# An attention and feed-forward block on one core: products moved in the steps of the last batch, the first transfers reordered

## The reference

```python
pos = 1.0 + x * (1.0 + 0.5 * x * (1.0 + x / 3.0))
neg = 1.0 / (1.0 - x * (1.0 - 0.5 * x * (1.0 - x / 3.0)))
s = where(x >= 0, pos, neg); attn = s / sum(s)     # x = logits - max(logits)
...
h = _layernorm(x) * (1 + ca) + sa
x = x + ga * attn(h)                               # q, k, v of 16 heads; times w_out, plus b_out
h = _layernorm(x) * (1 + cb) + sb
h = concat([h, -h]); h = relu(s0 * (h @ W0)) * 2   # 256 -> 512
h = relu(s1 * (h @ W1)) * 2                        # 512 -> 512
x = x + gb * s2 * (h @ W2)                         # 512 -> 128
```

## Time and profile before

| | before |
|---|---|
| median of 3 runs | 696.83 us (695.08 to 698.17) |
| profiled execution | 694.62 us, span 692.7 us, so 1.9 us lie outside the span |
| PE busy | 632.7 us (91%), 3065 matmuls |
| DVE busy | 641.2 us (93%), 757 instructions |
| ACT busy | 601.9 us (87%) |
| POOL busy | 598.8 us (86%) |
| DMA | 53.62 MB |

### The profile page before, as it was taken

The page is one execution under the profiler, slowest core; times in us unless marked ns, Lnnn a source line. Parts: engine busy times, 40 slices in busy tenths (PEclk is TensorE's granted clock), DMA queues, the critical chain, the costliest instruction groups (busy, mean ns, idle before and its releaser), DMA issues.

```text
span 692.7 us, 9651 instructions
## 1 busy us (share of the span) xinstructions
PE 632.7 (91%) x3065; PEld 253.7 (37%) x3065; DVE 641.2 (93%) x757; ACT 601.9 (87%) x622; POOL 598.8 (86%) x394
## 2 busy tenths in 40 slices
PE   6767998899889998999989998999989999998998
PEld 4223333334223343234423342234423343334366
DVE  6889999999999999999999999999999999998853
ACT  2587898998999989999999989998999989998932
POOL 8759888899989999999989999999989899797810
PEclk9588999999999999999999999999999999999999
DMA  8423112522214122512214122512214122101001
GB/s 230 159 67 132 53 51 61 168 63 59 63 53 154 32 58 72 174 55 59 77 47 156 37 58 70 176 55 59 75 51 160 32 58 72 52 10 28 16 13 31
DMA packets 37783, 53.62 MB, mean 77 GB/s; under 512 B 11308, under 2 KB 20804, under 8 KB 37732
## 3 DMA queue, kind: packets, MB, share of 16 engines
q1 hardware_dynamic: 36748, 51.81, 24.8%
q10 hardware_dynamic: 984, 1.19, 0.5%
HBM read 29.17 MB, written 18.36 MB: 69 GB/s over the span
## 4 chain that ended last, share of the span: by engine, by line
PE 56%; DVE 23%; issue 10%; ACT 9%; DMA 1%; ACTq 1%; DVEq 0%
PE MB L525 13%; PE OP L603 12%; DVE mx L988 11%; PE Z L571 9%; DVE cub L979 9%; PE SA L586 8%; ACT sq L736 4%; PE MB L538 3%; PE MB L515 2%; ACT prob L750 2%; PE MB L496 1%; ACT hid L843 1%; PE MB L503 1%; ACT hid L791 1%; DMA KH<-SK 1%
## 5 line engine op out<-in xcount | busy, mean ns | idle before, releaser
L1227 POOL TENSOR_TENSOR cub<-cub 128x2048 f32<-128x2048 f32 x127 | 456.8, 3603 | 39.7 <-DVE cub L979 39.4
L736 ACT ACTIVATE sq<-Z,shift 128x1024 f32<-128x1024 f32 x256 | 282.2, 1116 | 43.3 <-PE Z L571 41.8
L979 DVE SCALAR_TENSOR_TENSOR cub<-sq,Z 128x1024 f32<-128x1024 f32 x256 | 309.5, 1210 | 11.0 <-ACT sq L736 10.8
L988 DVE TENSOR_REDUCE mx<-SA 128x2 f32<-128x1024 f32 x248 | 301.7, 1216 | 13.4 <-PE SA L586 9.9
L750 ACT ACTIVATE prob<-cub 128x2048 f32<-128x2048 f32 x128 | 244.4, 1910 | 1.5 <-DVE cub L946 1.1
L586 PE MATMUL SA<-KH,QL 64*128 64x512 f32 x496 | 123.0, 492 | 30.9 <-DVE mx L988 25.3
L571 PE MATMUL Z<-QH,KH 64*128 64x512 f32 x512 | 128.9, 500 | 5.9 <-DVE cub L979 5.8
L603 PE MATMUL OP<-prob,Vq 128*16 128x512 f32 x1024 | 134.3, 598 | 0.0
L571 PEld LDWEIGHTS Z<-QH,KH 64*128 64x128 f32 x512 | 48.2, 185 | 181.8 <-DVE cub L979 124.1
L525 PE MATMUL MB<-hid,W 128*128 128x512 f32 x192 | 108.1, 645 | 0.0
L586 PEld LDWEIGHTS SA<-KH,QL 64*128 64x128 f32 x496 | 47.4, 187 | 111.5 <-DVE mx L988 85.1
(11 more groups left out here) (215 smaller groups left out, 522.5 us busy)
## 6 DMA issues: line engine op xcount, KB each, us to landing
QL<-parts_q SPq DMA_DIRECT2D x62, 128.0 KB, 2.6
KH<-parts_k SPq DMA_DIRECT2D x62, 128.0 KB, 2.7
QH<-parts_q SPq DMA_DIRECT2D x62, 128.0 KB, 2.7
parts_q<-SQ SPq DMA_DIRECT2D x28, 256.0 KB, 2.6
parts_k<-SK SPq DMA_DIRECT2D x28, 256.0 KB, 2.7
nd<-OT SPq DMA_DIRECT2D x124, 32.0 KB
QH<-mp SPq DMA_DIRECT2D x126, 4.0 KB
out<-y SPq DMA_DIRECT2D x7, 256.0 KB, 2.8
```

Of the source, the lines that this page charges most:

```text
L736: nc.scalar.activation(sq[:, h, :], Z[:, h, :], ACT.Square, bias=shift[:, 0:1]).then_inc(s_sq, 1)
L979: nc.vector.scalar_tensor_tensor(cub[:, m % RING, h, :], sq[:, h, :], CUB_ADD, Z[:, h, :], ALU.add, ALU.mult).then_inc(s_cv, 1)
L988: nc.vector.tensor_reduce(to, unit_bank(m, u)[:, :, :], AX_X, ALU.max).then_inc(s_mx, 1)
L1227: nc.gpsimd.tensor_tensor(ff, ff, ff, ALU.mult).then_inc(s_fp, 1)
```

## The change

In the lead-in: x is loaded in four parts in place of three, and the third (batches 4 and 5) moves behind the first quad and the writing of the parts of q, the fourth (6 and 7) behind the reading of quad 1. The first quad's QH transfers move ahead of the writing of q's parts. ACT waits for the parts of x one by one as it sums, leaves its two DMAs of the first rows of maxima to SP, and squares tiles in steps -2, -1, 2 and 3 in place of -3 to 0. POOL's `norms_of_x` of these moves from step 3 to step 5. PE gets 14 more matmuls without a reader before the first logits, and fills in steps 10 to 12 of the lead-in.

In the last batch's steps: the first layer of batch 6 is made in steps 11 and 12 (before 11 to 14), two of its products in banks of SA; the second layer in steps 13 to 15, its last product in steps 128 and 129 as before; half of `y` in step 130, before in the tail. Transposes of `h2T` move to the start of step 11, and DVE's `norm_late` to the end of its step. DVE reads out the first layer in steps 11 to 14 (before 12 to 15), and the last square is done half by DVE in step 127 and half by POOL. A fill less is made among the logits' fills.

```diff
--- before.py
+++ after.py
@@ -56,8 +56,8 @@
 AV_BEHIND = 5
 LOADS = 4
 ON_VECTOR = 3
-SQUARES_AT = (-3, -2, -1, 0)
-X_LOADS = (slice(0, 1), slice(1, 4), slice(4, B))
+SQUARES_AT = (-2, -1, 2, 3)
+X_LOADS = (slice(0, 1), slice(1, 4), slice(4, 6), slice(6, B))
 M_DMAS = 4
 LEAD = 3
 FIRST = -1
@@ -89,30 +89,31 @@
     ("l1_3", -2, [(6, "c", 1), (6, "d", 1), (7, "c", 1), (7, "d", 1)]),
     ("x1", -1, [(8, "b", 2), (8, "c", 2)]),
     ("y", -2, [(9, "b", 1), (9, "c", 1), (9, "d", 1), (10, "b", 1)]),
-    ("h2T", -1, [(10, "d", 4)]),
-    ("l0_0", -1, [(11, "c", 4)]), ("l0_1", -1, [(12, "c", 4)]), ("l0_2", -1, [(13, "c", 4)]), ("l0_3", -1, [(14, "c", 4)]),
-    ("l1_0", -1, [(13, "d", 1), (14, "d", 1), (15, "d", 1), (H, "c", 1)]),
-    ("l1_1", -1, [(13, "d", 1), (14, "d", 1), (15, "d", 1), (H, "c", 1)]),
+    ("h2T", -1, [(11, "a", 4)]),
+    ("l0_0", -1, [(11, "c", 4)]), ("l0_1", -1, [(11, "d", 4)]), ("l0_2", -1, [(12, "c", 4)]), ("l0_3", -1, [(12, "d", 4)]),
+    ("l1_0", -1, [(13, "c", 2), (14, "b", 1), (15, "b", 1)]),
+    ("l1_1", -1, [(14, "c", 2), (14, "d", 1), (15, "c", 1)]),
+    ("l1_2", -1, [(15, "c", 2), (15, "d", 2)]),
 ]
 
 MISC[B] = [
-    ("l1_3", -2, [(0, "b", 3), (0, "c", 1)]), ("l1_2", -2, [(2, "c", 4)]), ("y", -2, [(5, "c", 3), (5, "d", 1)]),
+    ("l1_3", -2, [(0, "c", 4)]), ("y", -2, [(2, "d", 2), (5, "c", 1), (5, "d", 1)]),
 ]
 
 
 
-FILL = {(FIRST, n): ("v", 1) for n in range(13, 16)}
+FILL = {(FIRST, n): ("v", 1) for n in range(10, 16)}
 FILL |= {(0, n): ("k", 2) for n in range(2, 11)} | {(0, n): ("v", 2) for n in range(12, 16)}
 FILL |= {(1, n): ("k", 3) for n in range(2, 8)} | {(1, n): ("x1", 1) for n in range(9, 11)} | {(1, 12): ("v", 3)}
 
-FILL_LOGITS = {(B - 1, n) for n in (10, 11, 12)}
+FILL_LOGITS = {(B - 1, 9), (B - 1, 10)}
 
 
 MAIN_AT = {"xbg": 6, "wog": 5, "den_sq": 6, "den_inv": 6, "att": 7, "st2": 9, "mv2": 10, "rs2": 11, "x1n": 11,
            "w2g": 0, "xn": 10}
 AT = {b: MAIN_AT for b in range(FIRST, B)}
 AT[B - 1] = MAIN_AT | {"st2": 9, "mv2": 9, "rs2": 9, "x1n": 10}
-AT[B] = MAIN_AT | {"xbg": 0, "wog": 0, "w2g": 1}
+AT[B] = MAIN_AT | {"w2g": 0, "xbg": 1, "wog": 1}
 
 
 
@@ -356,8 +357,10 @@
 
         own_bank = {product(FIRST, "k", 0): (SA[:, 0, :], None),
                     product(B - 1, "y", B - 3): (SA[:, 1, :], None),
-                    product(B - 1, "l1_0", B - 2): (SA[:, 0, :], None),
-                    product(B - 1, "l1_1", B - 2): (SA[:, 1, :], product(B - 1, "y", B - 3)),
+                    product(B - 1, "l0_1", B - 2): (SA[:, 0, :], None),
+                    product(B - 1, "l0_2", B - 2): (SA[:, 1, :], product(B - 1, "y", B - 3)),
+                    product(B - 1, "l1_0", B - 2): (SA[:, 0, :], product(B - 1, "l0_1", B - 2)),
+                    product(B - 1, "l1_1", B - 2): (SA[:, 1, :], product(B - 1, "l0_2", B - 2)),
                     product(B, "l1_3", B - 2): (Z[:, 1, 0:S], None),
                     product(B, "y", B - 2): (SA[:, 1, :], product(B - 1, "l1_1", B - 2))}
         common = [o for o in order if o not in own_bank]
...
@@ -577,6 +580,7 @@
                     return
                 beta, g, r, qt = logits_at(m, u)
                 if m == 0 and u == 0:
+                    without_reader(14)
                     pe.wait_ge(s_gate, 1)
                 if m % QUAD == 0 and u == 0:
                     pe.wait_ge(s_qk[g], loads_of_qk(beta, g) * 16)
@@ -621,7 +625,10 @@
             scores(s + 1, 0)
             misc("a")
             logits(m, 1)
-            with_v(s)
+            if s != GROUPS:
+                with_v(s)
+            if s == GROUPS - 1:
+                with_v(s + 1)
             misc("b")
             scores(s + 1, 1)
             misc("c")
@@ -670,7 +677,7 @@
                 if t % 2 == 1:
                     mm.then_inc(t_x1, 1)
             y_before = product(B, "y", B - 2)
-            misc_product(pe, *y_before, range(0, 3))
+            misc_product(pe, *y_before, range(2, 3))
             for t in range(TB):
                 pe.wait_ge(t_x1n, t + 1)
                 mm = nc.tensor.transpose(t_h2T_banks[t // 2][:, t % 2 * P:(t % 2 + 1) * P], x1n[:, t, :], ident[:, :])
@@ -740,7 +747,7 @@
                     if m < GROUPS - 1:
                         act.wait_ge(s_fp, m + 1)
                     else:
-                        act.wait_ge(s_last_fp, 1)
+                        act.wait_ge(s_last_fp, 2)
                     if m == 0:
                         act.wait_ge(s_wts, 2)
                         act.wait_ge(s_W0, 2)
@@ -827,14 +834,12 @@
                 write_parts(nc.scalar, "k", 0, OTHER_QUADS)
             if b == FIRST and n == 3:
 
-                for load in s_x[1:]:
-                    act.wait_ge(load, 16)
                 for i in range((B - ON_VECTOR) * TB):
+                    for j, load in enumerate(X_LOADS):
+                        if i == 0 and j == 1 or i == (load.start - ON_VECTOR) * TB:
+                            act.wait_ge(s_x[j], 16)
                     mm = nc.scalar.activation(scratch(i), tile_of_x(i), ACT.Copy, accum_out=sum1[:, i:i + 1])
                 mm.then_inc(s_sum1, 1)
-            if s == 4 - AHEAD:
-                act.wait_ge(s_mp, 1)
-                rows_of_maxima(nc.scalar, 0, range(2, P // 32))
             if s in SQUARES_AT:
                 if s == SQUARES_AT[0]:
                     act.wait_ge(s_mean1, 1)
@@ -941,8 +946,9 @@
             ones(KH, slice(1, 2))
 
         def last_square(dve):
+
             dve.wait_ge(s_cv, 2 * GROUPS)
-            ff = cub[:, (GROUPS - 1) % RING].rearrange("p a n -> p (a n)")
+            ff = cub[:, (GROUPS - 1) % RING, 1, :]
             nc.vector.tensor_tensor(ff, ff, ff, ALU.mult).then_inc(s_last_fp, 1)
 
         def sums_of(dve, quad):
@@ -1052,32 +1058,31 @@
             if m > QUAD:
                 of_maxima(m, 1)
             split(b, n)
-            if b == B - 1:
-                norm_late()
             cubic(s, 1)
             if m > QUAD:
                 of_maxima(m, 2)
             maxima(m, 1)
             if b < B - 1:
                 norm_sums()
+            else:
+                norm_late()
             if b == B - 1 and n in (8, 12):
                 sums_of(dve, (s - AV_BEHIND) // QUAD)
-            if b == B - 1 and n >= 12:
-                take_late(dve, b, f"l0_{n - 12}")
             if b == B - 1 and n == 11:
                 dve.wait_ge(s_made["y"], B - 2)
                 dve.wait_ge(s_out, 16 * (B - 3))
                 nc.vector.tensor_tensor(flat(y), bank_of(*product(b, "y", B - 3))[0], flat(xs[:, B - 3]), ALU.add)\
                     .then_inc(s_y, 1)
+            if b == B - 1 and 11 <= n < 15:
+                take_late(dve, b, f"l0_{n - 11}")
+            if b == B - 1 and n == 15:
+                last_square(dve)
             if b == B and n in (0, 4):
                 sums_of(dve, (s - AV_BEHIND) // QUAD)
             if b == B and n == 0:
-                last_square(dve)
-                take_late(dve, B - 1, "l1_0")
-                take_late(dve, B - 1, "l1_1")
+                for name in ("l1_0", "l1_1", "l1_2"):
+                    take_late(dve, B - 1, name)
                 take_late(dve, B, "l1_3")
-            if b == B and n == 2:
-                take_late(dve, B, "l1_2")
             if b == FIRST and n == 2:
                 stats_of_x(dve, 1)
                 means_of_x(dve, 1)
@@ -1221,7 +1226,11 @@
             b, n = s // H, s % H
 
             def square_of(m):
-                if 0 <= m < GROUPS - 1:
+                if m == GROUPS - 1:
+                    pool.wait_ge(s_cv, 2 * m + 1)
+                    ff = cub[:, m % RING, 0, :]
+                    nc.gpsimd.tensor_tensor(ff, ff, ff, ALU.mult).then_inc(s_last_fp, 1)
+                elif 0 <= m < GROUPS:
                     pool.wait_ge(s_cv, 2 * (m + 1))
                     ff = cub[:, m % RING].rearrange("p a n -> p (a n)")
                     nc.gpsimd.tensor_tensor(ff, ff, ff, ALU.mult).then_inc(s_fp, 1)
@@ -1301,7 +1310,7 @@
                 normalise_x(b + 2)
             if at(s, "x1n", -1, b, n) and b < B - 1:
                 normalise_x1(b - 1)
-            if b == 0 and n == 3:
+            if b == 0 and n == 5:
                 norms_of_x(pool, True)
             square_of(s)
 
@@ -1349,7 +1358,6 @@
             sp.dma_start(k0u, k0.rearrange("(a p) n -> p a n", p=P)).then_inc(ld_k, 16)
             sp.dma_start(k1u, k1.rearrange("(a p) n -> p a n", p=P)).then_inc(ld_k, 16)
             sp.dma_start(k2u, k2.rearrange("(a p) n -> p a n", p=P)).then_inc(ld_k, 16)
-            load_x(sp, 2)
         def sp_step(sp, s):
             b, n = s // H, s % H
 
@@ -1368,8 +1376,9 @@
                 if beta == 0:
                     sp.wait_ge(s_zero, 2)
                     first_quad(sp, QL, "q", s_qk[0])
+                    first_quad(sp, QH, "q", s_qh[0])
                     write_parts(sp, "q", 0, OTHER_QUADS)
-                    first_quad(sp, QH, "q", s_qh[0])
```

(4 more changed lines are left out.)

4 lines of the change are left out of this document (2 added, 2 removed).

## The result

The changed kernel takes 703.47 us in the median of 4 runs (702.89 to 706.65), the kernel before beside it 696.03 (695.08 to 698.17). The ratio is 1.0103 with a 95% interval of 1.0078 to 1.0128: slower by 1.0%, and outside the predicted range. The profiled execution has a span of 701.1 us, 692.7 before. PE is busy for 641.6 us, 632.7 before, DVE for 644.7, 641.2 before.

What follows compares the result with a forecast made beforehand. No one engine bounds the whole, its 128 steps run in series; at the end PE's own work bounds. Lead-in 0 and end +0.9 on 694.62 gave 695.5, plus 2.2 for the median: 697.7 us, range 694.0 to 700.8.

Steps and rivals of the forecast that it cites:

- x1n at 633.9 ... the first cubic of step 12 ... 2.1 us late: Last batch: x1n ends at 633.9 after POOL's square; DVE waits for l0_0, so that cubic starts at 641.5, before 639.38.
- The slower rival: Last batch: POOL's next square breaks up x1n, 2.4 us on top, +3.3 in all, 700.1 us; chance 0.2.
- PE's own work: The end: from step 15's values' product PE is the bound, 12.5 us to the last values' products, 11.8 before.
- the sum: Whole kernel: lead-in about 0 and end +0.9 us added to the profiled 694.62 us, giving 695.5; 697.7 for the median.
- 1.71 us of PE go for sure: The end: PE's wait of 1.71 us at 644.27 for a first-layer bank to be read out goes.
- the faster rival: Lead-in and end: x early or gate rows not delaying quad 2, end gaps closed; -2.7 us, 694.1 us; chance 0.2.
- gain of 0.2: Tail: y matmuls shrink to a third, but what follows waits for x1n on DVE, so only 0.2 us gained.
- 1.0 without cover: Last square: halving it gains nothing as PE is the bound behind it; without PE's cover it would give 1.0 us.
- The fills cost nothing: Lead-in: two pairs of logits at 0.43 and a fill of some 1.05 us stand against two maxima of 1.13 each.
- ten late squares: Lead-in, ACT: squares moved to steps 2 and 3 cost 0.2 us in step 2 and 1.3 more in step 3.
- its own bounds (-0.9 to +2.4): Lead-in: -0.9 us if x lands after 2.7 us, +2.4 if after 6.0 and nothing else gives way.
- its bound of 3.0: The end: 3.0 us later if y's two thirds and the 2.1 us late first cubic of step 12 add up.

Runs made afterwards that it cites:

- norm_early: Changed kernel with DVE's norm_late back ahead of the second cubic of its step, nothing else: 701.59 us, 1.0067.
- last_steps_only: Changed kernel with all lead-in edits undone, the last batch as changed: 701.49 us, 1.0065.
- both_mended: Changed kernel with x1n early, read-outs behind steps 12 and 13's cubics, y in the tail, q's parts ahead of QH, gate rows behind quad 2's read-back: 696.21 us.
- lead_parts_first: Kernel before with the lead-in's edits alone, but q's parts written ahead of the first quad's QH, as before: 698.74 us, 1.0028.
- lead_thin: As lead_parts_first, with the gate rows' write one step later and the ten late squares spread two in each of steps 2 to 6: 695.2 us, 0.9979.
- all_thin: As both_mended, with the ten late squares of x spread two in each of steps 2 to 6: 693.79 us, 0.9964.

## Why the prediction was wrong

**The forecast took the wrong case at x1n.** Its step was "x1n at 633.9 ... the first cubic of step 12 ... 2.1 us late", blocked by one square of POOL. The slower rival had it: POOL's second square was ready and ran between two of the four. The prediction had written that both cubics of step 122 were now ahead of x1n, so that POOL always had its next square ready; that was evidence, and I gave it 0.2 for lack of a row. The first cubic of step 12 came 6.2 us late (648.03, with the 2.5 us of the lead-in taken off), and 2.6 late in norm_early, where the square is out of the way: the rest of that step was about right. The rival's price, 2.4 us on top, was near: the timed runs give 2.5 and 2.7. The 3.6 us of the profiles are this and a longer stretch at half clock, in which l0_0 ran (DVE's wait for it 4.37 us, against 2.90); in last_steps_only, with a shorter one, it is 33.01 against 30.33, or 2.7.

**The moved products gain nothing by themselves.** This is the second step that failed, and the rival didn't have it. PE's own work was forecast well: 12.3 us from step 15's values' product where the sum had 12.5, with 1.5 us moved ahead (1.4 in the sum). But the steps ahead of it grew. Even with x1n early, the last batch alone would stand at 1.0043 (norm_early less the lead-in's 0.24%), some 3.0 us over, and the sum had 0.9. In the profiles the end is 1.8 us longer with x1n and the read-outs mended (29.96 against 28.12), where the sum had PE begin step 15's values' product 0.6 late. Counted from the last product of the scores, what is taken off PE is 2.0 us (14.2 to 12.2, with y in the tail); it comes back ahead of that product, where each step is a ring of PE's product, ACT's square and DVE's cubic. That the ring had no room left is how I read the rows: in both_mended PE waits four times for a cubic in these steps, 2.8 us in all. The "1.71 us of PE go for sure" of the faster rival fell with it.

**y was the avoidable part.** Its share stood in the sum, at 2.1 us (2.94 x 16/24 is 1.96), set off against the pieces moved; it measured 2.0. In the tail the same matmuls lie beside DVE's work (the tail is 27.1 us with them or without, at full clock), so the "gain of 0.2" in the tail was nothing. The halved last square gave nothing, as said, but "1.0 without cover" was also wrong: 2.66 us for half beside GpSimd, 2.31 for the whole.

**The lead-in: right string, wrong length.** The steps were those of the sum, each later: quad 1's reading at 24.12, not 22.0; x's last part issued at 27.84, not 25.7, and 4.12 us to land, not 3.6; means at 34.52, not 32.0; gate rows at 40.21, not 37.5; K at 44.97, not 42.4. The first miss is the write of q's parts, which the reading waits for: its last issue ends at 21.50, and the reading starts 2.6 us behind that, where I had 22.0. The wait for quad 1's K that this makes, 2.68 us, was not in the sum; by lead_parts_first it isn't what cost. (The 1.3 MB of x that the prediction names for batches 4 to 7 are 1.0 MB; nothing was worked out from it.) The start came out well: the 28 instructions took 3.29 us, the clock was 1.00, and the first maximum stood at 18.69, not 18.0. "The fills cost nothing" held, though not for the reason given (a fill takes 2.07 at half clock): they lay in a wait for quad 1's K, which the sum did not have. For the ten late squares 1.5 us was forecast; DVE waited 1.10 at 65.64, and spreading them gained 1.0 (lead_thin) and 1.5 us (all_thin) by the ratios, with intervals that overlap.

**The sum.** Forecast 0 and +0.9; measured alone, 0.24% or 1.7 us and 0.65% or 4.5 us, together 7.4. The lead-in's loss lies within its own bounds (-0.9 to +2.4), the end's lies outside its bound of 3.0. Not settled: 1.2 us of these 7.4 that the two halves do not add up to (within their intervals), and why the same wait of PE in the same code is followed by half clock in two of seven profiles.
